# DLRM tower: a new order of stores, loads, evictions and unread products in step 0

## The reference, cut to what matters

```python
xk = x0
for W in (W0, W1, W2):          # W: (32, h_prev, 64); h_prev = 32, 64, 64
    xk = relu(einsum('bmd,bhd,mhk->bkd', x0, xk, W))
    outs.append(sum(xk, axis=2))            # 64 sums per sample and layer
h = concat([concat(outs), dense_ctx])       # 192 + 16 numbers
y = relu(relu(h @ W_top1 + b_top1) @ W_top2 + b_top2) @ W_top3
```

## Time and profile before

| what | value |
|---|---|
| median of 3 runs | 1159.43 us (1157.27 to 1159.99) |
| the profiled execution | 1160.98 us, its span 1157.9 us |
| TensorE busy | 1102.0 us, 95% of the span |
| VectorE busy | 1093.0 us, 94% |
| ScalarE busy | 972.5 us, 84% |
| GpSimd busy | 906.4 us, 78% |
| chain that ended last | PE 83%, DVE 6%, ACT 5%, issue 2%, DMA 2%, POOL 1% |

### The profile page before, as it was taken

One profiled execution on the slowest core, in us unless ns is written; L12 is line 12 of the kernel. 1 busy time (PEld: TensorE's weight loads), 2 busy tenths in 40 slices (PEclk: granted clock), 3 DMA queues, 4 the chain that ended last, 5 costly groups with the idle time before them and its releaser, 6 DMA issues.

```text
span 1157.9 us, 18022 instructions
## 1 busy us (share of the span) xinstructions
PE 1102.0 (95%) x5396; PEld 388.6 (34%) x5396; DVE 1093.0 (94%) x477; ACT 972.5 (84%) x4487; POOL 906.4 (78%) x637
## 2 busy tenths in 40 slices
PE   0788999999999999999999999999999999999998
PEld 0332223333333333333333333333333333333333
DVE  1699999999999999999999999999999999999994
ACT  0364549998999989998999989999899989999863
POOL 6757888888888888888888888888888888885310
PEclk9999999999999999999999999999999999999999
DMA  7697677866667886666788666678866667886100
GB/s 177 158 189 160 152 153 170 177 143 142 140 142 153 171 177 140 145 141 143 149 173 173 141 144 135 147 153 177 169 145 148 138 146 145 177 175 145 34 1 0
DMA packets 78770, 167.47 MB, mean 145 GB/s; under 512 B 22121, under 2 KB 39810, under 8 KB 78674
## 3 DMA queue, kind: packets, MB, share of 16 engines
q1 hardware_dynamic: 59616, 157.78, 62.4%
q0 software_dynamic: 16384, 4.23, 3.7%
q10 hardware_dynamic: 2674, 4.34, 1.7%
HBM read 157.88 MB, written 8.40 MB: 144 GB/s over the span
## 4 chain that ended last, share of the span: by engine, by line
PE 83%; DVE 6%; ACT 5%; issue 2%; DMA 2%; POOL 1%; ACTq 0%; SPq 0%; DVEq 0%
PE acc L989 77%; DVE p_dve L858 4%; PE acc L1092 4%; ACT xb L547 2%; POOL x_rows L458 1%; ACT out_l L631 1%; DVE p_dve L874 1%; ACT xb L527 1%; ACT x_s L535 1%; DMA spread<-x_of_steps 1%; DMA x_rows<-in_table,ids_s 1%; PE acc L1099 1%; PE acc L1129 0%; DVE z L901 0%; PE acc L1137 0%
## 5 line engine op out<-in xcount | busy, mean ns | idle before, releaser
L989 PE MATMUL acc<-p_dve,w_s 128*64 128x512 f32 x3780 | 841.2, 595 | 18.9 <-DVE p_dve L858 18.1
L458 POOL DMA_INDIRECT x_rows<-in_table,ids_s x512 | 492.4, 962 | 146.6 <-issue 132.3
L858 DVE TENSOR_TENSOR p_dve<-spread,xb 128x3072 f32<-128x3072 f32 (+2 forms) x222 | 557.9, 2571 | 2.2 <-PE acc L989 2.2
L858 DVE TENSOR_TENSOR p_dve<-spread,xa 128x2048 f32<-128x2048 f32 (+1 forms) x189 | 488.0, 2638 | 12.6 <-ACT xa L541 6.1
L989 PEld LDWEIGHTS acc<-p_dve,w_s 128*64 128x64 f32 x3780 | 269.5, 137 | 555.9 <-issue 481.2
L470 POOL TENSOR_TENSOR p_l<-spread,q_tile 128x2048 f32<-128x2048 f32 x58 | 263.6, 4569 | 13.3 <-DMA q_tile<-x_of_steps 10.1
L547 ACT ACTIVATE xb<-x_s 32x1024 f32<-32x1024 f32 x240 | 244.6, 1019 | 20.0 <-DVE p_dve L858 17.1
L486 POOL TENSOR_TENSOR p_pool<-spread,x_s 128x1024 f32<-128x1024 f32 x63 | 150.2, 2384 | 58.8 <-PE acc L989 51.1
L535 ACT ACTIVATE x_s<-acc 64x512 f32<-64x512 f32 x252 | 148.6, 590 | 52.8 <-PE acc L989 49.9
L631 ACT ACTIVATE out_l<-out_l 128x16 f32<-128x16 f32 x896 | 178.1, 200 | 0.7
L619 ACT ACTIVATE out_l<-out_l 128x16 f32<-128x16 f32 x896 | 177.5, 199 | 0.0
(11 more groups left out here) (46 smaller groups left out, 312.2 us busy)
## 6 DMA issues: line engine op xcount, KB each, us to landing
spread<-x_of_steps SPq DMA_DIRECT2D x242, 512.0 KB, 16.9
q_tile<-x_of_steps SPq DMA_DIRECT2D x120, 128.0 KB
x_rows<-in_table,ids_s POOLq DMA_INDIRECT x512, 4.5
x_of_steps<-x_rows SPq DMA_DIRECT2D x60, 128.0 KB
spread<-x_of_steps SPq DMA_DIRECT2D x10, 256.0 KB, 6.2
spread<-x_of_steps ACTq DMA_DIRECT2D x6, 256.0 KB, 7.5
w_s<-in_w SPq DMA_DIRECT2D x2, 512.0 KB, 7.1
spread<-x_of_steps SPq DMA_DIRECT2D x8, 128.0 KB, 3.3
```

Source lines behind the costliest of these rows:

```text
L458: nc.gpsimd.indirect_dma_start(out=x_rows[:, s % 2, i * DIM:(i + 1) * DIM], out_offset=None, in_=table, in_offset=bass.IndirectOffsetOnAxi ...
L858: nc.vector.tensor_tensor(p_dve[:, to:to + n, :], spread[:, s % 3, tile:tile + n, :], over(x[:], n), ALU.mult).then_inc(dve_made, n)
L989: last = nc.tensor.matmul(halves(acc[b * K:(b + 1) * K, :]), w, of_block(prod, b), start=start, stop=stop)
```

## The change

In five places, all within step 0:

```diff
-L0_OF_HALF_1_BEFORE = 6
+L0_OF_HALF_1_BEFORE = 11
-BUSY_BEHIND = 4
+BUSY_AHEAD, BUSY_BEHIND = 7, 2
...
-            for b in range(2):
-                store_half_by(sp, 0, b, x_stored)
-                sp.wait_ge(x_stored, 32 * (b + 1))
-                load_half(0, b, SP_QUADS)
+            store_half_by(sp, 0, 0, x_stored)
+            sp.wait_ge(x_stored, 32)
+            load_half(0, 0, SP_QUADS)
+
+            store_half_by(sp, 0, 1, x_stored)
+            load_b_of_0_by(sp, 0, half_b_loaded)
+            sp.wait_ge(x_stored, 64)
+            load_half(0, 1, SP_QUADS)
+            store_half_by(sp, 1, 0, x_stored)
             load_b_of_0_by(sp, 1, b_loaded[0])
-            store_half_by(sp, 1, 0, x_stored)
             sp.wait_ge(x_stored, 96)
...
                 if h == 0:
+
+                    act.wait_ge(x_stored, 64)
+                    load_half_by(act, 0, 1, ACT_QUADS)
                     half_squares(0, 1)
...
             load_half_by(act, 0, 0, ACT_QUADS)
-            load_b_of_0_by(act, 0, half_b_loaded)
             half_squares(0, 0)
-            act.wait_ge(x_stored, 64)
-            load_half_by(act, 0, 1, ACT_QUADS)
             act.wait_ge(w_loaded, LOADED)
...
             pe.wait_ge(w0_ready, 3)
+            keep_busy(acc1[1], BUSY_AHEAD)
             layer0_half(acc0, 0, 0)
             keep_busy(acc1[1], BUSY_BEHIND)
```

## The result

| | before | changed |
|---|---|---|
| median | 1158.13 us (1155.12 to 1160.86, 20 runs) | 1160.61 us (1158.12 to 1162.74, 20 runs) |
| profiled execution | 1160.98 us, span 1157.9 | 1158.12 us, span 1156.3 |
| ratio to before | | 1.0021, 95% interval 1.0013 to 1.0028 |

The change makes the kernel 2.5 us (0.2%) slower, where 4.8 us faster was forecast. The two profiled executions don't show that: before's is 2.9 us above its median, the changed kernel's is the fastest of its 20. So I compare marks inside the traces first, and whole times by medians.

The account below looks back on a forecast made before the run. TensorE and VectorE were 95 and 94 per cent busy, so only the dense part's start could move: -5.3 + 0.3 + 0.2 = -4.8 us, from 1159.43 to 1154.6 us; 8-in-10 range 1151.5 to 1159.0.

Parts of the forecast that it names:

- Part 1: Step 0: with "b" of half 0 out of the gathers' way, the store of half 1 comes 4.9 us earlier.
- Part 2: Step 0: half 0 starts earlier, VectorE's tiles (0,3) at 32.0 instead of 37.80, 5.8 us, not all kept.
- Part 3: Rest of half 0, what is late next: start of half 1's tiles moves from 50.67 to 45.4, 5.3 us.
- rival A: "b" of half 0 lands late, (3,3) at 38.2 instead of 34.3, total 1158.5 us; chance 0.23.
- so q lands right behind "b", 34.8: SyncE's queue in step 0: q of half 1 lands at 34.8, squares to 35.4, `xb` to 38.35, (8,3) at 38.4.
- Part 5: Unread products in step 0: seven ahead end at 21.9, cost nothing; a faster clock is worth 0, 1.5 us at most.
- the forecast's mark: Start of half 1's tiles on VectorE in step 0, forecast at 45.4 us instead of 50.67.
- TensorE 1.1 us behind: First layer of half 1: VectorE's products end at 42.5, TensorE at 43.6, `xa` of half 1 at 45.1.
- rivals B and C: B, the clock: shifted work misses a slow stretch, 1152.1 us (chance 0.12), or meets one more, 1157.1 us (0.08).
- Rival C: TensorE's clock never rises in step 0, 8.5 us later, total 1163.1 us; chance 0.07.
- Part 4: After half 1's start, whether the gain stays: 0.3 us charged for late "b" of half 1, 0.2 for the rest.
- the forecast's signs of being wrong: Last gather near 30, "b" after 37, VectorE waiting for `spread` before 90 us, slow records after 40, GpSimd's first product late.

Follow-up runs that it names:

- loads ahead: Changed kernel with ScalarE's wait for the store and its six loads of half 1 back ahead of the `xa` eviction: 1157.57 us, ratio to before 0.9992.
- q first: Changed kernel with SyncE's two q loads of half 1 issued ahead of the four "b" loads of half 0: 1158.5 us, ratio to before 1.0013.
- `xb` first: Changed kernel with ScalarE evicting `xb` of half 0 ahead of the squares of half 1: 1156.03 us, ratio to before 0.9993.
- the twelve executions: The changed kernel run again, unaltered, for a second trace: 1160.13 us against 1157.5, ratio to before 1.0025.

## Why the prediction was wrong

**Part 1 was right.** Store of half 1 issued at 25.98 (25.9 forecast), x stored at 29.2 or before (28.4; loads that wait for it were issued at 28.4 to 28.6 in loads ahead and q first).

**Part 2 was right within a microsecond.** VectorE's first layer 25.59 (24.5), `xa` evicted from 31.43 (30.5), tiles (0,3) 32.99 (32.0).

**Part 3 holds the step that failed.** "b": (3,3) at 35.35 (34.3), close; rival A did not come. The step is "so q lands right behind 'b', 34.8": q was there at 38.7, 3.9 us later. The sentence looked at SyncE's two quads of q alone. ScalarE's two had been moved behind the `xa` eviction as well, which I had even put at 30.5 when I let ScalarE's loads join then, and I never asked when the q among them lands. They are issued at 31.5 to 31.9, into the traffic. The squares stand on all four quads, `xb` on the squares: 4.0 us on tiles (8,3) (42.39 against 38.4).

How the 3.9 us divide: with ScalarE's loads issued first of all (loads ahead) q is there at 36.3, so 1.5 us are a landing amid "b" and "a" that I had put too early. With them behind the eviction and the full clock (`xb` first) it is 36.7, 0.4 us more. The last 2.0 us come with the low clock at 27 to 31, which delays the eviction and so the loads. Part 5 gave the faster clock a worth of 0, because (3,3) waits for "b"; it followed that path and not this one. These are single traces, so the parts are sizes of one execution each.

Taking `xb` off the wait for q gives the forecast's mark (44.84), and the version is 4.1 us faster than the changed kernel in the same job. That is shown. Loads ahead has a ratio to before of 0.9992 against 1.0021 and 1.0025 of the changed kernel, 3.4 to 3.8 us, measured in different jobs.

The rising 5.7 to 9.2 us of the earlier trace rows, which the forecast read as landing in the order of issue, are four loads on one semaphore, so that order is how the profile books them. What a place behind "b" costs is shown by q first: 1.9 to 2.0 us ahead of it, 5.4 and 6.5 behind it.

**Part 3, the first layer of half 1.** "TensorE 1.1 us behind" assumed the full clock. The hole that the late q opens (39.5 to 44.2) is followed by 1.2 GHz, and TensorE ends 3.1 us behind VectorE, as against 1.5 in `xb` first. VectorE's wait for `xa` is 1.96 us, as against 0.28 there: 1.7 us for the clock. 45.4, 4.0 later at (8,3), 0.2 shorter from there to the end of (14,2), and the wait of 1.96 give 51.2, the mark measured.

**Part 5 and rivals B and C.** The seven products ran from 15.9 to 24.4 us, not to 21.9, before "a", and cost nothing there. Their records of 512 columns are 0.85 us apart at the start and 0.43 later. The forecast's 0.43 was twice a record of 256 columns at the low clock; that it is the cost at the full clock is luck. Rival C had the right kind of cause, a clock that falls when TensorE waits in step 0, but asked only whether it would rise; it had 0.07. Of the stretches that the changed kernel's trace has and before's has not, the one at 44 to 48 is a loss; the one at 27 to 31 is new in the granted clock alone, as before's records were slow there too. The mean granted clock is 0.991 in the median of the changed kernel's 20 executions and 0.996 in before's 35.
The Trainium skill ("TensorE: Matmul & The Clock Gate", section "Part 1: The HAM clock gate (the "warmup" mystery)") says that the array is throttled by default, that activity releases it and idleness throttles it again, at moments not tied to the program. The trace agrees: the unread products start at 0.85 us a record, low stretches stand behind the holes of 3.1 us at 25 and 4.7 us at 40, and a hole of 3.7 us near 25 was followed by none in `xb` first, so they differ between executions.

**Part 4 was not tested by the change**, since the mark never moved. `xb` first tests it, and it was too low: 1.95 us of waiting within half 1 instead of 0.3, and at step 1's first layer 0.55 us of waiting for `spread` and 2.2 us by which one product was longer while GpSimd's ran, where 0.2 stood for all of that. So of a lead of 5.8 us at the mark 0.9 were left at 73 us, without a wait of VectorE for TensorE. Of the forecast's signs of being wrong this is the wait of VectorE for `spread` before 90 us.

**What stays open.** The traces give +0.5 and +1.2 us at the mark, the medians +2.5. Both traces are of executions faster than their medians. That the slower ones have a lower mean clock is what the twelve executions say; no trace shows where. Whether the seven products ahead bring some of it is not settled. In six traces with them the first layer ran at the full clock in two (1.95 us) and at the low one in four.

## What to carry to other kernels

When loads are moved behind a wait, list every transfer among them with its reader, the small one on the shortest path first: here 256 KB of q, half of it behind "b" and half behind an eviction, came 3.9 us late, though 1 MB of "b" came in time. A load that stands behind an eviction inherits every delay of the work that the eviction waits for. And a hole made in TensorE's work is priced with the clock that follows it.

## What was not expected of the hardware

A granted clock of 0.5 lasted 3 to 10 us each time, and in every trace of the usual condition there were two to five such stretches. Six of the seven have one among the first steady steps; there the one at 95 to 100 costs 1.7 us. The clock also read 1.00 at 29 to 33 in the kernel before while its records ran at half speed, so a granted clock is to be checked against the length of the records. A product of VectorE took 3.38 us instead of 1.22 while a product of GpSimd ran (`xb` first, 69.8 us). The same chip ran the same kernel before at 1157.5 us in one job and at 1273.3 in another.
